# Attention scores in 64-row tile pairs that telescope over the key tiles, ordered scores, maxima, scores, maxima

## What is computed

```python
def _L0_attn_ref(X, W_qkv, b_qkv, W_fc, b_fc):
    B, L, E = (4, 256, 128)
    H, DK = (16, 64)
    b, l, _ = X.shape
    qkv = X @ W_qkv + b_qkv
    qkv = qkv.reshape(b, l, H, 3 * DK).transpose(0, 2, 1, 3)
    Q, K, V = jnp.split(qkv, 3, axis=-1)
    scores = jnp.einsum('bhqd,bhkd->bhqk', Q, K) / np.sqrt(DK).astype(np.float32)
    attn = jax.nn.softmax(scores, axis=-1)
    out = jnp.einsum('bhqk,bhkv->bhqv', attn, V)
    out = out.transpose(0, 2, 1, 3).reshape(b, l, H * DK)
    return out @ W_fc + b_fc
...
h = _layernorm(x, axis=-1) * (1 + ca) + sa
x = x + ga * _L0_attn_ref(h, ...)
h = _layernorm(x, axis=-1) * (1 + cb) + sb
x = x + gb * _L0_ffn_ref(h, ...)
```

## Time and profile before

| what | us |
|---|---|
| median of 3 runs | 1919.35 |
| lowest and highest | 1916.85 to 1920.01 |
| the profiled execution | 1920.44 |
| its span, first to last instruction | 1918.7 |
| setup, until the attention's first product | 44.1 |
| attention, from there to its last DVE instruction | 1647.4 |
| router and experts, after it | 227.2 |

### The profile page before, as it was taken

How to read it: one execution, slowest core, us unless ns; L and a number is a source line. 1 busy time by engine, 2 the same in 40 slices (tenths; PEclk the granted TensorE clock), 3 DMA queues, 4 the chain that set the end, 5 groups by cost and what they waited for, 6 DMA issues and landing times. The chain is left out here.

```text
span 1918.7 us, 29207 instructions
## 1 busy us (share of the span) xinstructions
PE 1813.9 (95%) x7819; PEld 991.3 (52%) x7819; DVE 1313.7 (68%) x2687; ACT 1051.4 (55%) x1944; POOL 1169.5 (61%) x521
## 2 busy tenths in 40 slices
PE   4799999999999999999999999999999999946996
PEld 3444555555555555455555555555555555434886
DVE  5777666666666666666666666666666666467788
ACT  3455555555555555555555555555555555414874
POOL 4466666667666666666766666666667666711124
PEclk8899999999999999999999999999999999956999
DMA  2111111111111111111111111111111111020010
GB/s 84 50 45 50 45 50 47 46 44 50 50 42 41 49 50 50 49 45 43 50 50 50 44 49 48 45 50 47 47 44 50 50 39 40 18 72 22 26 36 28
DMA packets 81217, 87.96 MB, mean 46 GB/s; under 512 B 27773, under 2 KB 50842, under 8 KB 81178
## 3 DMA queue, kind: packets, MB, share of 16 engines
q1 hardware_dynamic: 81024, 87.47, 16.6%
q10 hardware_dynamic: 154, 0.03, 0.0%
HBM read 31.35 MB, written 2.36 MB: 18 GB/s over the span
## 5 line engine op out<-in xcount | busy, mean ns | idle before, releaser
L581 POOL TENSOR_TENSOR ACC<-ACC,PR 128x1024 f32<-128x1024 f32 x382 | 924.6, 2420 | 256.0 <-ACT PR L638 255.1
L666 DVE TENSOR_REDUCE NMH<-ps_mx 128x1 f32<-128x512 f32 x1016 | 693.1, 685 | 491.6 <-PE ps_mx L827 487.1
L638 ACT ACTIVATE PR<-ps_s 128x512 f32<-128x512 f32 x1024 | 556.0, 595 | 617.1 <-PE ps_s L841 612.7
L850 PE MATMUL ps_o<-PR,V 128*64 128x512 f32 x2048 | 548.9, 614 | 0.0
L827 PE MATMUL ps_mx<-KA,QA 128*128 128x512 f32 x1016 | 456.7, 450 | 8.7 <-DVE NMH L666 8.2
L840 PE MATMUL ps_s<-QA,KA 128*128 128x512 f32 x1024 | 408.7, 399 | 0.0
L841 PE MATMUL ps_s<-QB,KB 128*128 128x512 f32 x1024 | 403.4, 394 | 0.0
L827 PEld LDWEIGHTS ps_mx<-KA,QA 128*128 128x128 f32 x1016 | 190.9, 188 | 407.4 <-issue 202.2
L581 POOL TENSOR_TENSOR ACC<-PR 128x1024 f32<-128x1024 f32 x64 | 161.9, 2530 | 278.8 <-ACT PR L638 278.8
L841 PEld LDWEIGHTS ps_s<-QB,KB 128*128 128x128 f32 x1024 | 192.7, 188 | 44.5
L850 PEld LDWEIGHTS ps_o<-PR,V 128*64 128x64 f32 x2048 | 106.9, 135 | 207.2 <-issue 105.0
(11 more groups left out here) (187 smaller groups left out, 1519.8 us busy)
## 6 DMA issues: line engine op xcount, KB each, us to landing
hcur<-hT SPq DMA_DIRECT2D x32, 512.0 KB, 3.6
KA<-KA SPq DMA_DIRECT2D x128, 128.0 KB, 2.3
QB<-QA SPq DMA_DIRECT2D x128, 128.0 KB, 2.2
SUM<-recip_rows SPq DMA_DIRECT2D x128, 128.0 KB, 2.9
Wraw<-in_L_attn_W_qkv SPq DMA_DIRECT2D x32, 192.0 KB, 2.4
x<-in_L_attn_X SPq DMA_DIRECT2D x4, 512.0 KB, 5.3
Wfc<-in_L_attn_W_fc SPq DMA_DIRECT2D x32, 64.0 KB, 1.8
R<-SUM SPq DMA_DIRECT2D x128, 2.0 KB, 1.8
```

What stands on the lines that cost most here:

```text
L581: G.tensor_tensor(ACC[:, ch, :, :], a, PR[:, t, :, :], ALU.add).then_inc(added, 1)
L638: A.activation(PR[:, t, h, :], ps_s[:, h, :], ACT.Exp, scale=SCALE).then_inc(exp_done, 1)
L666: D.tensor_reduce(NMH[:, ch, h, i, kc:kc + 1], banks[:, kc, :], AX, ALU.max, negate=True).then_inc(mx_red, 1)
L850: last = T.matmul(ps_o[half(h), ch, :], V[:, u, t, half(h)], PR[:, t, h, :], start=(t == 0), stop=(t == 7))
```

## The change

The attention stage is written anew around blocks of two steps; the other stages are not touched.

- **Tiles.** Each product of the scores and the maxima now has 64 rows: head 0 on partitions 0 to 63, head 1 on 64 to 127, issued one behind the other into different banks. The scores of a step and both heads are three such pairs of products (hi by `QH`, `DL` by `QH`, hi by `QL`) where there were four of full height; the maxima of a group are one pair where there were two products for each head and query tile.
- **Telescoping.** The bank `ps_s[:, t % 2]` is not started afresh for t of 2 and more: `DH` and `DL` hold the two parts of the difference between key tile t and key tile t-2, and the products add it to what stands in the bank. So the negative maxima (`BQ` against `one_r`) are added at t = 0 and 1 alone.
- **Banks.** `ps_s` 4 (two steps by two heads), `ps_mx` 2 (one for each head), `ps_o` 1, `ps_w` 1.
- **Maxima.** A group k is (half, query tile, key half) for both heads. `maxima` waits for both reductions of the group before it. `rows` writes into `ps_mx` too.
- **Order.** A block d of eight in a pair is, on PE: scores 2d, maxima k, scores 2d+1, maxima k+1, at d = 3 and 5 the sums, `times_v` of the two steps of the block before, at d = 3 and 7 `rows`, one unit of the table `LATE`.
- **Exponentials.** One ACT instruction for both heads (128x1024).
- **K and Q.** ACT reads K into `Kraw`, DVE subtracts within `ps_w` to get the differences (`k_step`), ACT rounds them into `DH`, DVE writes `DL`. Q needs one ACT and one DVE instruction. `dup_k` and `dup_q` are gone.
- **Output.** ACT copies `ps_o` to `O` (`copy_o`), DVE then multiplies `O` by `SUM` in place.

```diff
-        QA = sb("QA", [P, 2, 2, L], F32R)
-        QB = sb("QB", [P, 2, 2, L], F32R)
-        KA = sb("KA", [P, 2, 2, L], F32R)
-        KB = sb("KB", [P, 2, 2, L], F32R)
+        QH = sb("QH", [P, 2, L], F32R)
+        QL = sb("QL", [P, 2, L], F32R)
+        KH = sb("KH", [P, 2, L], F32R)
+        DH = sb("DH", [P, 2, L], F32R)
+        DL = sb("DL", [P, 2, L], F32R)
+        Kraw = sb("Kraw", [P, L])
...
-        ps_s = psum("ps_s", [P, 2, 512])
+        ps_s = psum("ps_s", [P, 2, 2, 512])
         ps_mx = psum("ps_mx", [P, 2, 512])
-        ps_o = psum("ps_o", [P, 2, 512])
-        ps_w2 = psum("ps_w2", [P, 2, 512])
...
+        ps_o = psum("ps_o", [P, 512])
+        ps_w = psum("ps_w", [P, 512])
...
+        LATE = {0: ("k", 1, 0), 1: ("k", 1, 1), 2: ("q", 1, 0), 3: ("q", 1, 1), 4: ("v", 1, 0), 5: ("fc", -1, 1),
+                6: ("v", 1, 1), 7: ("fc", 0, 0)}
+        SUMS = {3: (-1, 1), 5: (0, 0)}
+        RECIP = {4: (-1, 1), 6: (0, 0)}
+        NORM = {5: (-1, 1), 7: (0, 0)}
...
+            def early_part(kind, m, u, ch):
                 q = slice(ch * 512, ch * 512 + 512)
...
+                if kind == "k":
+                    act.wait_ge(k_proj, 2 * m + ch + 1)
+                    A.activation(Kraw[:, q], ps_w[:, :], ACT.Identity, bias=bias[:, u, 1:2]).then_inc(k_raw, 1)
+                elif kind == "q":
+                    act.wait_ge(q_proj, 2 * m + ch + 1)
+                    A.activation(QH[:, u, q], ps_w[:, :], ACT.Identity, bias=bias[:, u, 0:1]).then_inc(q_hi, 1)
...
+            def late_part(kind, m, u, ch):
+                if kind != "k":
+                    return
+                q = slice(ch * 512, ch * 512 + 512)
+                new = slice(256 - 256 * ch, 512)
+                act.wait_ge(k_raw, 2 * m + ch + 1)
+                A.activation(KH[:, u, q], Kraw[:, q], ACT.Copy)
+                act.wait_ge(k_step, 2 * m + ch + 1)
+                A.activation(DH[:, u, ch * 512 + new.start:ch * 512 + 512], ps_w[:, new], ACT.Copy).then_inc(k_hi, 1)
...
+            def copy_o(m, ch):
+                act.wait_ge(pv_done, 16 * m + 8 * ch + 8)
+                wait(act, fc_mm, 2 * m + ch - 1)
+                A.activation(O[:, ch, :], ps_o[:, :], ACT.Copy).then_inc(o_copied, 1)
...
+            def exponentials(n, s):
+                ch, t = divmod(s, 8)
+                wait(act, pv_done, 16 * n + s - 7)
+                wait(act, added, 7 * (2 * n + ch - 1) + max(t, 1))
+                act.wait_ge(scored, 16 * n + s + 1)
+                A.activation(PR[:, t, :, :], ps_s[:, t % 2, :, :], ACT.Exp, scale=SCALE).then_inc(exp_done, 1)
...
+            def reduce_max(m, u, ch, i, kc, count):
+                if i == 0 and kc == 0:
                     wait(dve, mx_both, 2 * m + ch - 1)
-                for kc in range(2):
-                    dve.wait_ge(mx_done, 2 * count - 1 + kc)
-                    D.tensor_reduce(NMH[:, ch, h, i, kc:kc + 1], banks[:, kc, :], AX, ALU.max, negate=True).then_inc(mx_red, 1)
-                if h == 1 and i == 3:
-                    dve.wait_ge(mx_red, 2 * count)
+                for h in range(2):
+                    dve.wait_ge(mx_done, 2 * count + h + 1)
+                    D.tensor_reduce(NMH[:, ch, h, i, kc:kc + 1], ps_mx[:, h, :], AX, ALU.max, negate=True).then_inc(mx_red, 1)
+                if i == 3 and kc == 1:
+                    dve.wait_ge(mx_red, 2 * count + 2)
                     wait(dve, rows_t, 2 * m + ch - 1)
-                    D.tensor_tensor(NM[:, ch, :, :], NMH[:, ch, :, :, 0], NMH[:, ch, :, :, 1], ALU.min).then_inc(mx_both, 1)
...
+                    D.tensor_reduce(NM[:, ch, :, 0:4], NMH[:, ch, :, :, :], AX, ALU.min).then_inc(mx_both, 1)
+            def mask_rows(m, ch):
+                dve.wait_ge(rows_t, 2 * m + ch + 1)
+                wait(dve, scored, 16 * m + 8 * ch - 8)
+                rows = ps_mx[:, 0, 0:P].unsqueeze(1).to_broadcast([P, 4, P])
+                D.tensor_tensor(BQ[:, ch, :].rearrange("p (i q) -> p i q", i=4), rows, mask[:, :, :], ALU.mult).then_inc(neg_rows, 1)
...
                 if kind == "k":
-                    dve.wait_ge(k_hi, 2 * m + ch + 1)
-                    for h in range(2):
-                        last = D.tensor_tensor(KB[half(h), u, h, q], raw[half(h), ch, :], KA[half(h), u, h, q].bitcast(F32), ALU.subtract)
-                    last.then_inc(k_lo, 1)
+                    dve.wait_ge(k_raw, 2 * m + ch + 1)
+                    new = slice(256 - 256 * ch, 512)
+                    D.scalar_tensor_tensor(ps_w[:, new], ps_w[:, new], bias[:, u, 1:2], Kraw[:, 256 * ch:256 + 512 * ch],
+                                           op0=ALU.add, op1=ALU.subtract).then_inc(k_step, 1)
...
+                    D.scalar_tensor_tensor(QL[:, u, q], ps_w[:, :], bias[:, u, 0:1], QH[:, u, q].bitcast(F32),
+                                           op0=ALU.add, op1=ALU.subtract).then_inc(q_lo, 1)
...
+                dve.wait_ge(k_hi, 2 * m + ch + 1)
+                if ch == 0:
+                    D.scalar_tensor_tensor(DL[:, u, 0:256], ps_w[:, 0:256], bias[:, u, 1:2], KH[:, u, 0:256].bitcast(F32),
+                                           op0=ALU.add, op1=ALU.subtract)
+                new = slice(256 - 256 * ch, 512)
+                k = slice(ch * 512 + new.start, ch * 512 + 512)
+                D.tensor_tensor(DL[:, u, k], ps_w[:, new], DH[:, u, k].bitcast(F32), ALU.subtract).then_inc(k_lo, 1)
...
             def normalise(m, ch):
                 dve.wait_ge(recip_in, 32 * (2 * m + ch + 1))
-                dve.wait_ge(pv_done, 16 * m + 8 * ch + 8)
-                wait(dve, fc_mm, 2 * m + ch)
-                D.tensor_tensor(O[:, :], ps_o[:, ch, :], SUM[:, :], ALU.mult).then_inc(o_norm, 1)
+                dve.wait_ge(o_copied, 2 * m + ch + 1)
+                D.tensor_tensor(O[:, ch, :], O[:, ch, :], SUM[:, ch, :], ALU.mult).then_inc(o_norm, 1)
...
-                wait(pe, mx_red, 2 * (count - ahead) - 1 + kc)
...
+            def rows(m, ch):
+                pe.wait_ge(mx_both, 2 * m + ch + 1)
+                T.matmul(ps_mx[:, 0, 0:P], NM[:, ch, :, :].rearrange("p h j -> p (h j)"), ident_r[:, :],
+                         start=True, stop=True).then_inc(rows_t, 1)
...
+            def maxima(m, u, ch, i, kc, count):
+                if kc == 0:
+                    pe.wait_ge(q_hi, 2 * m + ch + 1)
+                if ch == 0 and i == 0:
+                    pe.wait_ge(k_hi, 2 * m + kc + 1)
+                wait(pe, mx_red, 2 * count)
                 q = ch * 512 + i * P
-                T.matmul(banks[:, kc, :], QA[:, u, h, q:q + P], KA[:, u, h, kc * 512:(kc + 1) * 512],
-                         start=True, stop=True).then_inc(mx_done, 1)
+                for h in range(2):
+                    T.matmul(ps_mx[:, h, :], QH[half(h), u, q:q + P], KH[half(h), u, kc * 512:(kc + 1) * 512],
+                             start=True, stop=True).then_inc(mx_done, 1)
...
+                hi = KH if t < 2 else DH
                 if t == 0:
                     pe.wait_ge(neg_rows, 2 * n + ch + 1)
-                    pe.wait_ge(qdup[u][ch], 32 * (n // 2) + 32)
+                    pe.wait_ge(q_lo, 2 * n + ch + 1)
                     if ch == 0:
                         pe.wait_ge(k_lo, 2 * n + 2)
+                wait(pe, exp_done, 16 * n + s - 1)
+                if t < 2:
+                    for h in range(2):
+                        T.matmul(ps_s[:, t, h, :], one_r[half(h), :], BQ[half(h), ch, :], start=True, stop=False,
+                                 skip_group_check=True)
                 for h in range(2):
-                    wait(pe, exp_done, 32 * n + 2 * s + h - 1)
-                    T.matmul(ps_s[:, h, :], KA[:, u, h, k], QA[:, u, h, q], start=True, stop=False)
-                    T.matmul(ps_s[:, h, :], KB[:, u, h, k], QB[:, u, h, q], start=False, stop=True).then_inc(scored, 1)
+                    T.matmul(ps_s[:, t % 2, h, :], hi[half(h), u, k], QH[half(h), u, q], start=False, stop=False,
+                             skip_group_check=True)
+                for h in range(2):
+                    T.matmul(ps_s[:, t % 2, h, :], DL[half(h), u, k], QH[half(h), u, q], start=False, stop=False,
+                             skip_group_check=True)
+                for h in range(2):
+                    last = T.matmul(ps_s[:, t % 2, h, :], hi[half(h), u, k], QL[half(h), u, q], start=False, stop=True,
+                                    skip_group_check=True)
+                last.then_inc(scored, 1)
...
+                for d in range(8):
+                    k = 2 * d + 9
+                    scores(n, u, 2 * d)
+                    if has(group(n, u, k)[0]):
+                        if d % 4 == 0:
+                            pe.wait_ge(neg_rows, 2 * n + d // 4 + 1)
+                        maxima(*group(n, u, k), 16 * n + k)
+                    scores(n, u, 2 * d + 1)
+                    if has(group(n, u, k + 1)[0]):
```

(26 more changed lines are left out.)

383 lines of the change are left out of this document (160 added, 223 removed).

## The result

| | before | after |
|---|---|---|
| median of 4 runs each, us | 1919.68 | 1958.45 |
| lowest and highest | 1916.85 to 1920.41 | 1953.27 to 1961.77 |
| the profiled execution | 1920.44 | 1957.91 |
| its span | 1918.7 | 1956.2 |

The ratio is 1.0202, 95% interval 1.0177 to 1.0227: the changed kernel is 2% slower (the interval does not tell a little under 2% from a little over), 7 us from the 1965 forecast.

A forecast was written before the change was run, and what follows sets the result against it. PE's own work bounded the kernel before; after, PE waits on DVE between maxima and at block 7's rows. 31 x (51.77 - 50.34) = +44, +4, -3: +45 on 1920.4, so 1965 us, range 1880 to 2030.

The forecast's parts named there:

- The slot: Scores and maxima on PE: two 64-row products of different heads run abreast in 0.233 us, upper end 0.27.
- The rival of serial products: Scores and maxima on PE: 64-row products don't run abreast, slot 0.47, time 2190 us; chance 0.07.
- The changes of form: PE between 64-row products and the others: 0.10 us on entering the 64-row form, 0.08 on leaving to `times_v`.
- The faster bound with free changes: Going between 64-row and 128-row forms costs nothing: 0.18 x 8 x 31 = 45 us less, range down to 1920.
- The wait: Between a block's two maxima: at least 1.75 us through DVE's reductions, PE has 0.93 to do, stands 0.8 a block.
- DVE's instructions on K and Q: Blocks 1 to 4: `k_step` or `QL` on DVE comes before the reductions; blocks forecast at 5.84, 6.10, 7.24, 6.12 us.
- The port: Block 7: DVE's `normalise`, both operands in SBUF, is locked out by POOL until 5.27; block 7.80 us, pair 51.77, without it 50.01.
- the rival without the lock: `normalise` slips in ahead of POOL: pair 50.01, 1911 us; with free changes of form too, 1866; chance 0.20.
- The longer serial chain: Loop register instructions behind waits, or DVE's bias instructions blocked by POOL: +1 to 2 us a pair, 2010 to 2040; chance 0.09.
- The prologue: From first product to first scores: 26.6 us before, near 31 after, +4, with nine groups of maxima at some 1.95.
- The last pair: End of the attention: the last pair lacks half of the maxima, its stalls are gone, -3 us.
- The signs: Profile after: pair 51 to 53 us, PE idle 0.8 to 1.3 before second maxima, 1.5 or more at block 7's `rows`.

The follow-up runs named there:

- split order: Against the kernel with the multiplication on POOL and second maxima behind `times_v`: in blocks 3 and 7 these maxima stay ahead of `times_v`; 1809.10 us, ratio 0.9434.
- between, with the multiplication on DVE: Against the 1790.88 us kernel (multiplication on POOL, second maxima between the two `times_v`): multiplication of O by SUM back on DVE; 1841.11 us, ratio 0.9607.

## Why the prediction was right

The pair was forecast at 51.77 and took 51.50. Block by block, from the starts of the first scores in PE's timeline:

| block | 0 | 1 | 2 | 3 | 4 | 5 | 6 | 7 |
|---|---|---|---|---|---|---|---|---|
| predicted | 5.95 | 5.84 | 6.10 | 7.24 | 6.12 | 6.80 | 5.92 | 7.80 |
| measured | 5.99 | 5.76 | 6.02 | 7.17 | 6.19 | 6.78 | 5.96 | 7.63 |

- **The slot.** 0.233 for two 64-row products, taken from `times_v`: 0.23 measured. The rival of serial products is out.
- **The changes of form.** Between products of full height and 64-row products 0.10 is lost on leaving and 0.10 on entering (701.77 to 702.10 and 702.10 to 702.43, 0.33 each in place of 0.23), much as between column forms. The faster bound with free changes is out.
- **The wait.** From maxima to maxima 1.75 forecast, 1.78 in block 1, and it moves with what is put between: the experiments with the maxima behind or between show it as the cause, the one that waits for each bank alone shows that it is the length of two reductions.
- **DVE's instructions on K and Q** in blocks 1 to 4: right within 0.08, and seen once more where extra work of PE was free in blocks 2 and 3.
- **The port.** L684 was walked at 2.57 (2.7 to 5.27) and took 2.44; the rival without the lock (1911) is what the kernel with the multiplication elsewhere measures, 1910.5.
- **The longer serial chain.** This rival had DVE's instructions with a bias operand blocked by POOL too. They are not: the 64 that write `QL` take 0.735 to 0.752 us, though 31 of them overlap an instruction of POOL.
- **What was mis-sized.** The sum was 44 for the pairs, +4 and -3. From the starts of the scores in the two traces, the 31 distances between pairs add up to 1599.5 and 1565.4, +34.1. The forecast had the pair too long (51.77 for 51.60), and took the one before from a single distance (50.34, where the mean is 50.50): 10 too much. The prologue: +4 forecast; from the first product to the first scores after takes 34.2 (43.32 to 77.55) where before took 26.6, +7.6. Its nine groups of maxima come 2.43 apart and not 1.95: the granted clock of this stretch is 0.50 throughout (0.69 before), a slot is 0.42 to 0.43, two maxima with nothing but the chain between them are 2.2 apart, and those with a V unit between 2.7. The last pair was to give back 3 and gives back nothing: from its first scores to the attention's last DVE instruction 55.9 after, 55.4 before. But the router and the experts, which the change does not touch, take 223.3 where they took 227.3, -4.0: the same 1092 products of PE, at a granted clock of 0.87 against 0.84. No run was made to test whether the clock is the cause. With the attention's beginning 0.7 earlier this is 34.1 + 7.6 + 0.4 - 4.0 - 0.7, the 37.5 of the span to rounding. So the mechanism was right; that the time came within 7 us is in part luck, since errors of -10, +4, +3, -4 and -1 partly cancel.
- **The signs.** The pair, the reductions ahead of the second maxima and the multiplication came as listed. The wait at the rows was to be 1.5 or more and is 1.39; two thirds of the waits at the second maxima are booked at 0.43 to 0.70, under the 0.8 listed, since 0.16 of each stands in the product before. And a stretch at 1.2 GHz in the attention was named as a sign against the forecast: there is one in the loop, at 1005 us, which loses 1.7 us, and the prologue runs at 1.2 GHz throughout, where before it did so for part of its time.

## What to carry to other kernels

When an engine that is always busy is given less to do, look first for what runs on another engine between two of its instructions: here a chain of 1.75 us through DVE had been covered by work that the change removed or moved, and the order scores, maxima, scores, maxima left 0.93 to cover it. Put the work that is left between the two ends of the chain before anything else is judged; the same tiles, the same telescoping and the same products gave 1958 in one order and 1750 in another, with the multiplication of `O` and the two subtractions for `Wlo` moved to another engine. And see to it that a VectorE instruction with two SBUF operands does not stand, beside a busy GpSimd, ahead of something that TensorE waits for: 1.5 us a pair here for one that takes 0.68 by itself. Another, of 0.56, was worth 0.6 a pair when it was moved.

## What the runs showed of the hardware

- Six 64-row products issued head by head take three slots, as in pairs (1959.9 us against 1958.5).
- A wait of PE of 2.17 us, in a stretch otherwise full, was followed by a stretch at the 1.2 GHz level that cost 1.7 us, in 30 pairs; waits of 1.38, twice in a pair, in over half of them; one wait of 1.5 to 1.8 in each pair (split order), six times; one of 1.6 (between, with the multiplication on DVE), five times; one of 1.39 with shorter ones about it, once in the loop. What decides between them is not settled.
- DVE's multiplication with both operands in SBUF took from 0.68 to 2.88 us, by where it fell against POOL's additions; on POOL itself the same took 1.27, and in the kernels that have it there PE waited for it once, 0.3 us.
- DVE's instructions with one operand in PSUM, one in SBUF and a bias in SBUF took 0.735 to 0.752 us in all 64 cases (`QL`), 31 of which overlap an instruction of POOL.
